# A fused attention and feed-forward kernel on one Trainium2 core: the attention stage's batch loop written out

## What is computed

```
xn  = layernorm(x)
out = x + attention(xn) + ffn(xn)

attention: qkv = xn @ w_qkv; windows of 4 rows, one every 2 rows (511 a batch);
           8 heads of 64; softmax(q k^T / sqrt(512)) v in each window;
           y = o @ w_out + b_out, scattered back by addition (a row is in up to two windows)
ffn:       q4(h) @ q4(w_down)^T,  h = silu(q4(xn) @ q4(w_gate)^T) * (q4(xn) @ q4(w_up)^T)
           q4: blocks of 16 rounded to the FP4 grid, times the block's scale; 1408 hidden channels
```

## Time and profile before

| | |
|---|---|
| Median of 3 runs | 2278.43 us (2278.31 to 2281.01) |
| The profiled execution's own time | 2275.91 us |
| Its span, from the first to the last instruction | 2274.1 us |
| PE busy | 2160.4 us (95%) |
| DVE, POOL, ACT busy | 1638.1, 1220.4, 655.9 us (72%, 54%, 29%) |
| Mean clock granted to PE | 0.988 |
| Instruction transfers (queues q8, q14) | 1.62 MB and 0.17 MB |

### The profile page before, as it was taken

How to read it: one execution, slowest core, us unless ns; L and a number is a source line. 1 busy time by engine, 2 the same in 40 slices (tenths; PEclk the granted TensorE clock), 3 DMA queues, 4 the chain that set the end, 5 groups by cost and what they waited for, 6 DMA issues and landing times.

```text
span 2274.1 us, 46572 instructions
## 1 busy us (share of the span) xinstructions
PE 2160.4 (95%) x16704; PEld 1041.8 (46%) x16704; DVE 1638.1 (72%) x3097; ACT 655.9 (29%) x1007; POOL 1220.4 (54%) x880
## 2 busy tenths in 40 slices
PE   1899999999999987999999999999999999999998
PEld 0454444444444443444444444444444444444443
DVE  5587667666767555787787778778778777777774
ACT  1233334243333322222222222222222322222221
POOL 2166566566756444555555555555555555555552
PEclk9999999999999998999999999999999999999999
DMA  7547565664647427333333333433333333333332
GB/s 231 162 106 184 122 176 143 158 154 131 177 114 184 118 89 222 63 85 84 81 84 84 87 85 79 91 81 84 84 81 84 84 84 83 82 82 83 84 73 66
DMA packets 447373, 251.81 MB, mean 111 GB/s; under 512 B 365251, under 2 KB 371907, under 8 KB 447253
## 3 DMA queue, kind: packets, MB, share of 16 engines
q1 hardware_dynamic: 445860, 244.88, 43.9%
q10 hardware_dynamic: 1104, 4.19, 0.5%
q0 software_dynamic: 288, 0.94, 0.1%
HBM read 98.98 MB, written 59.77 MB: 70 GB/s over the span
## 4 chain that ended last, share of the span: by engine, by line
PE 59%; DVE 1%; POOL 0%; DMA 0%; issue 0%; POOLq 0%; ACT 0%; SPq 0%; DVEq 0%
PE dn L1235 13%; PE gu L1220 7%; PE gu L1224 7%; PE gu L1225 7%; PE gu L1222 7%; PE gu L1221 7%; PE gu L1223 7%; PE dn L1237 6%; POOL hv L169 0%; DMA ht<-hh 0%; DVE hv L205 0%; DVE hv L203 0%; POOLq L989 0%; DVE hv L1116 0%; DVE hs L179 0%
## 5 line engine op out<-in xcount | busy, mean ns | idle before, releaser
L904 PE MATMUL acc<-late 128*128 128x512 f16 x2304 | 527.8, 386 | 79.3 <-DMA late<-xh 56.0
L1235 PE MATMUL dn<-late,ht 128*128 128x512 f16 x1408 | 429.9, 380 | 5.3 <-DMA ht<-hh 5.3
L904 PEld LDWEIGHTS acc<-late 128*128 128x128 f16 x2304 | 221.4, 99 | 351.6 <-issue 99.7
L1116 DVE SCALAR_TENSOR_TENSOR hv<-gu,row_gains,sg 128x512 f32<-128x512 f32 (+1 forms) x192 | 129.0, 672 | 279.0 <-ACT sg L1180 279.0
L169 POOL TENSOR_TENSOR hv<-hv,hs 128x1408 f32<-128x1408 f32 x64 | 165.8, 2590 | 230.0 <-DVE hv L205 230.0
L1220 PE MATMUL gu<-late,turned 128*128 128x512 f16 (+1 forms) x768 | 277.9, 362 | 7.3 <-PEq L223 6.9
L1221 PE MATMUL gu<-late,turned 128*128 128x512 f16 (+1 forms) x768 | 277.8, 362 | 0.0
L1223 PE MATMUL gu<-late,turned 128*128 128x512 f16 (+1 forms) x768 | 277.8, 362 | 0.0
L1224 PE MATMUL gu<-late,turned 128*128 128x512 f16 (+1 forms) x768 | 277.8, 362 | 0.0
L1225 PE MATMUL gu<-late,turned 128*128 128x512 f16 (+1 forms) x768 | 277.8, 362 | 0.0
L1222 PE MATMUL gu<-late,turned 128*128 128x512 f16 (+1 forms) x768 | 277.8, 362 | 0.0
(11 more groups left out here) (124 smaller groups left out, 3258.7 us busy)
## 6 DMA issues: line engine op xcount, KB each, us to landing
late<-in_L_attn_x SPq DMA_DIRECT2D x64, 256.0 KB, 3.6
normed<-late SPq DMA_DIRECT2D x64, 256.0 KB, 2.4
res<-in_L_attn_x SPq DMA_DIRECT2D x64, 256.0 KB, 2.9
attended<-res SPq DMA_DIRECT2D x64, 256.0 KB, 2.5
raw<-normed SPq DMA_DIRECT2D x64, 256.0 KB, 2.7
pr<-attended SPq DMA_DIRECT2D x64, 256.0 KB, 2.7
out<-fo SPq DMA_DIRECT2D x64, 256.0 KB, 2.0
ready<-turned SPq DMA_DIRECT2D x36, 256.0 KB, 2.3
```

Of the source, the lines that this page charges most:

```text
L904: last = pe.matmul(out, lhsT, rhs, start=(at == 0), stop=(at == n - 1))
L1235: last = pe.matmul(dps[k][:, :], ht[:, k, at], w_hi, start=(at == 0), stop=(at == 2 * FC - 1))
```

## The change

`batches` no longer makes a hardware loop: it runs through all eight batches in Python, so that b is a number everywhere. With it go the registers for b, the waits against registers, the `hold` increments in the attention stage and the tests whether b is a number. A step marked "*" is emitted where it was. The order of the steps on each engine stays.

```diff
 def follow(steps, do, b, looped=False):
     for step in steps.split():
         c = b + step.count("+") - step.count("'")
-        if (looped or "*" not in step) and (not isinstance(c, int) or 0 <= c < B):
+        if (looped or "*" not in step) and 0 <= c < B:
             do[step[0]](c, int(step[1:].strip("+'*")))
 
-def batches(engine, first, second, do):
-
-    follow(first, do, -1)
-    follow(second, do, -1)
-    follow(first, do, 0)
-    with engine.Fori(0, LOOP) as b:
-        follow(second, do, b, True)
-        follow(first, do, b + 1, True)
-    follow(second, do, B - 2)
-    follow(first, do, B - 1)
-    follow(second, do, B - 1)
+def batches(first, second, do):
+
+    for b in range(-1, B):
+        follow(first, do, b, 0 < b < B - 1)
+        follow(second, do, b, 0 <= b < LOOP)
     follow(first, do, B)
...
-        held = [sem(f"held_{e}") for e in ("dve", "pe", "pool", "sp")]
...
             def load(b, i):
                 sp.wait_ge(xn_done, at(b, TPB, i - TPB))
-                hold(sp, held[3])
                 sp.dma_start(xb[:, i, :], x_t[b * TPB + i]).then_inc(x_in[i], 16)
...
             def turn_rows(b, i):
 
                 sp.wait_ge(xlo_done, at(b, TPB, i))
-                hold(sp, held[3])
                 sp.wait_ge(qkv_done, at(b, QKV, v_use(i) // 12 * 12 + 11 - QKV))
-                hold(sp, held[3])
                 sp.dma_start_transpose(xt[:, :, :, i * P:(i + 1) * P].rearrange("p a k t -> p (a k) t"),
                                        xh[:, i % 4].rearrange("p a c -> p (a c)")).then_inc(xt_in[i % 4], 16)
...
             def load_maxima(b, n):
 
-                if isinstance(b, int) and b == 0:
+                if b == 0:
...
                 pe.wait_ge(masked, at(b, NG, g - 1))
-                hold(pe, held[1])
```

More of the change, by code:

```diff
@@ L387, in turn_first @@
             def turn_first(b, k):
-                if isinstance(b, int) and b == B - 1:
+                if b == B - 1:
                     sp.wait_ge(rows.q["low"], k + 1)
@@ L468, in first_edge @@
                         .then_inc(ve_zero, 16)
-            batches(sp,
+            batches(
                     "r5' L5'* r6' l0+ S2'* l1+ k4 l2+ e0 l3+ k5 s3' T3'* l4+ Z6' S3'* Z7' r7' e1 k6 s4' k7 Z8' s5' "
@@ L503, in root @@
                 pool.wait_ge(mv_done, at(b, TPB, 4 * g + 3))
-                hold(pool, held[2])
                 pool.tensor_scalar(ln[:, r, 0], mv[:, r, 1], EPS, None, ALU.add).then_inc(ln_step, 1)
@@ L574, in _ @@
             pool.wait_ge(half_set, 1)
-            batches(pool,
+            batches(
                     "X4'* b6' w0 w1 r0+ O4'* o7' b7' W1+ l0+ l1+ l2+ l3+ X5'* w2 O5'* b0",
@@ L603, in weights @@
             def weights(b, n):
-                if not isinstance(b, int) or b != 0:
+                if b != 0:
                     return
@@ L648, in statistics @@
                 dve.wait_ge(stats, at(b, TPB, i))
-                hold(dve, held[0])
                 dve.bn_aggr(mv[:, i, :], st[:, i, :]).then_inc(mv_done, 1)
@@ L797, in unit_gains @@
                     dve.wait_ge(m_step, 5)
-            batches(dve,
+            batches(
                     "u0 z0 R4'* f4' t0+ t1+ t2+ t3+ f5' W0+ d7' R5'* g1 w0 f6' n0+ n1+ n2+ w1 n3+ t4+ t5+ W1+ m1 M0+ "
@@ L886, in first_high @@
                     high(act, rows.q, rows.raw[:, k, :], rows.split, k)
-            batches(act,
+            batches(
                     "B5'* q13 W0+ H4'* h7' W1+ q14 q15 W2+ v4 x0+ x1+ o0 x2+ x3+ o1 H5'* e1 v5 W3+ v6 v7",
@@ L977, in weights_ready @@
                         pe.wait_ge(ve_zero, 16)
-            batches(pe,
+            batches(
                     "p6' v4 s1 a0 v5 a1 p7'",
```

2 lines of the change are left out of this document (removed).

## The result

| | before | after |
|---|---|---|
| Median | 2278.37 us (2277.78 to 2281.01, 4 runs) | 2300.24 us (2294.69 to 2310.91, 4 runs) |
| Ratio | | 1.0102, 95% interval 1.0081 to 1.0122 |
| Span of the profiled execution | 2274.1 us | 2308.7 us |

The forecast was 2246.4 us, faster with 0.92. The kernel is slower by 1.0%, outside the range. The profiled execution of after is the slowest of its four (2310.91 us), so sums made from its trace come out some 10 us above the median.

The account below looks back on a forecast made before the run. PE bounds the kernel, busy 95% of the span. Branches' 32 us less 1 for late transposes gave 31, or up to 33 and more; 32 was taken from the median 2278.43, giving 2246.4 us, range 2242 to 2260.

Parts of the forecast that it names:

- Longer code: Attention stage: more instruction blocks fetched in straight order; PE's issue waits at scores 0 to 0.5 a lap, taken as 0.
- no effect: Rival, attention stage: the straight instruction stream starves where the branch stalled, idle spreads out; 2278 us, chance 0.03.
- the branch's loss comes back as issue waits elsewhere: Sign against the forecast: PE's idle at the loop branch reappears as instruction waits at other places; no size given.
- PE's taken branches: Attention loop's edges on PE: five taken branches go, gaining 32 us, or 6.4 an edge.
- SP's row: SP's transfers in attention: cheaper groups, 0.15 us each, issue the residual load r2 2.9 us earlier.
- What is late next: Attention laps: other engines must follow PE 6.4 us earlier; charged 0.2 a lap, 1 us, with SP's row shorter.
- my three places: Possible late spots in a lap: a3 fits by 1.0 us, d0 1.6 late without SP's gain, q8+ just in time.
- Registers and holds at zero: Attention stage on PE, DVE, ACT and POOL: removing register arithmetic and holds gains nothing, costed at zero.
- The slower rival, feed-forward: Feed-forward loop moved into three instruction blocks, one too many; 27 branches cost 6.4 each, 2419 us, chance 0.05.
- The ends: Batch 0 and the last, already written out, and PE's 6.86 us before feed-forward stay as they are.

Follow-up runs that it names:

- shift_24_and_12: The after kernel with 24 unused semaphore increments on PE before its first matmul and 12 more per batch; 2245.67 us, ratio to before 0.9865.
- loop_shifted_45: The before kernel, loop kept, with 45 semaphore increments on PE ahead of the batches; 2259.53 us, ratio to before 0.9925.
- slow_sync_queue_4: shift_24_and_12 with four unused semaphore increments on SP behind the first wait of each of its nine kinds of step; 2251.91 us.
- holds_back_on_PE: The after kernel with the 12 holds a batch put back on PE alone, behind the waits of scores and attend; 2294.27 us, ratio to before 1.0072.
- loop_shifted_205: The before kernel, loop kept, with 205 semaphore increments on PE ahead of the batches; 2318.26 us, ratio to before 1.0192.
- shift_76_and_12: The after kernel with 76 unused semaphore increments on PE before its first matmul and 12 more per batch; 2242.76 us, ratio to before 0.9843.
- shift_0_and_12: The after kernel with 12 unused semaphore increments per batch on PE and none ahead of its first matmul; 2296.67 us, ratio to before 1.0082.

## Why the prediction was wrong

**The step that failed is "Longer code".** It took "0 as in that batch, the only sample without a branch", and kept 0.5 a lap, 2.5 us, for the range. Measured in that profile: 36.1 + 2.7 + 2.3 = 41.1 us of issue waits up to 880 us, 1 to 3.7 at a time, and behind 12 of the 17 over 1 us a step wholly or partly at 1.2 GHz. The 59.2 us between the seven laps of after and of shift_24_and_12 are nearly all of the 68.0 between their spans; the rest is 2.9 ahead of the first v6 and some 5.3 behind the last. The batch from 739 to 836 us was no sample of straight code; it was a sample of one placement, and it happened to be a good one. The signs were there: small issue waits only at the scores, the densest stretch of instructions, and a block count that I did use, for feed-forward alone. Five of those six waits in before stand at one place, behind 136 pairs of s1, 272 instructions, where its second edge lies (17 + 256).

**The rival "no effect"**, given 0.03, had the right mechanism ("the straight stream starves where the branch stalled") but the wrong size, and its test was wrong: it asked whether ten blocks in 97 us are too many on average, where what counts is 384 instructions in 1.75 us. "The forecast is wrong if ... the branch's loss comes back as issue waits elsewhere" came true.

**PE's taken branches, 32 us:** they went. In a good place the time comes out as forecast: laps of 97.0 to 97.9 against the 96.97 that it used, 2245.67 against 2246.4 us. That is partly luck, since the term is less the branch's own than I thought: loop_shifted_45 keeps the branches and wins 18.9 of it. From there to slow_sync_queue_4, straight code with SP at the loop's pace, are 7.6 us by the medians and 11 by the ratios to before, 1.5 to 2.2 an edge. That is an estimate of what five taken branches cost by themselves, from two kernels that also differ in place.

**SP's row, 2.9 us shorter:** k0+ to r2 went from 26.4 to 24.0 us in shift_24_and_12, 2.4 shorter, and to 23.0 in after, with single transfers 0.48 apart. **What is late next:** without the shorter row I had 8 us for five laps; at the loop's pace the laps show 6.6 us. The size is about right, and so are the waits, for DVE's finished rows and for late<-xh. The copies ve<-v, which bite as SP gets slower still, were not among my three places. In shift_24_and_12 q8+ waits 1.3 us in all, where I charged 1.

**Registers and holds at zero:** right, as holds_back_on_PE shows for PE's holds: its time goes by its place; for the other engines no run tests it alone, but laps of 97 us leave no room for a loss. **The slower rival, feed-forward:** refuted. By the same count its loop body, some 430 instructions, lies in two blocks in before and in three in after; yet the branch stays at 208 ns and q8 moves nothing from 1050 to 2150 us. So three blocks were not too many. **The ends:** the 6.86 us stayed (6.91), but the last batch, written out in both, lost 5 us between v6 and feed-forward, through the 3.68 us stall above: code that the diff doesn't touch was moved too.

The Trainium skill (Runtime: NRT & Kernel Launch, "Instruction fetch mechanics") says that instructions come in 16 KiB blocks of 256, the next fetched while the current one runs, and that the cost of crossing is mostly hidden. The size agrees with the stalls 256 instructions apart. "Mostly hidden" holds for projections (24 instructions in 2.7 us) and not for badly placed scores, where a crossing cost 1 to 3.7 us and mostly the clock too. It also gives the stalls at taken branches as one reason to prefer full unrolling; here the unrolled kernel was slower by 1.0% in its first place and faster by 1.4% in a better one.

**What stays open.** Whether PE asks for one block ahead exactly is inferred from where the stalls stand and when the transfers start; which block a transfer brings, no trace says. The lower bound of the bad distances is approximate: s1 at 40 didn't stall and s2 at 44 did, but in batch 0 of after s2 took 4.13 us at 240, and s1 3.31 at 35. The upper bound depends on what follows. At 130 s0's second edge lies just behind its end, and PE stalled 2.71 us ahead of p1; s0 at 143 and s2 at 136 or more ran through into projections. Behind s1 come the short matmuls of a0, and there distances of 132 to 187 still cost 0.7 to 1.6 us, in a0. Why the good kernels differ among themselves (2242.8 to 2250.0) was not followed up; the fastest of them has its first s0 at 113 and loses 2.8 us there. No kernel was tried that spreads the scores' matmuls among projections, which would take away the burst.

## What to carry to other kernels

Where an engine executes some hundreds of short instructions in a microsecond or two, count how far the burst begins from the next edge of a 256-instruction block: a step of 384 wants the edge within its first 40, or so far behind that the second edge, 256 on, falls past the end of the step and of the short steps that follow it. Any edit ahead of it, unrolling above all, moves that edge, so try a change in several places (some no-ops ahead of the loop) before you judge it: the same written-out code ran at 2243 to 2300 us, the loop code at 2260 to 2318. A stretch without waits is a sample for other code only if its instructions lie alike.

## What the runs showed of the hardware

- Between two whole programs that differ in no-ops alone, the placement of code made 2.6% (loop_shifted_45 and loop_shifted_205); the change under study made 1.0%.
- A pause of 2 to 3 us in PE's stream can cost as much again: the twelve matmuls of the next projection took 5.30 us instead of 2.76. Behind 12 of the 17 stalls of after (pauses of 1.69 to 3.68 us) they took 3.7 to 5.3 us, behind the other five (1.05 to 2.11) 2.76. In the seven laps of after the slow clock made 24.4 of 59.2 us.
- The time of a kernel with such stalls can vary from run to run: after spreads over 16 us in four runs (0.7%), shift_76_and_12 over 2.9; but shift_0_and_12, with as many stalls, over 4.5.
- A branch to a target that isn't there takes PE 4.07 to 4.43 us in either place, but shows as an idle of 1 to 2 us, since queued matmuls cover the rest. The dear part in before was the block edge right behind its target.
- On SP, two increments beside a transfer were nearly free (0.48 to 0.51 us from one transfer to the next; the transfer's own record fell from 0.44 to 0.34), and further ones cost 0.06 each.
